# Attention state and ratio products of layer 0 over the value columns of their own half of the heads

## What is computed

```
Q = elu(xn @ wq.T + bq) + 1        K = elu(xn @ wk.T + bk) + 1        V = xn @ wv.T + bv
KV    = einsum('bhsd,bhse->bhde', K, V)       # per head: 16 x 16, summed over 512 tokens
K_sum = sum of K over the tokens              # per head: 16
out   = (Q @ KV) / (Q @ K_sum + 1e-8)         # per head
x    += out @ wo.T + bo + experts(xn)
```

## Time and profile before

| | |
|---|---|
| median of the runs | 1319.93 us |
| profiled execution, span | 1318.2 us |
| around the span (median less span) | 1.7 us |
| PE busy | 97% of the span |
| DVE, ACT, POOL busy | 60%, 40%, 10% |
| PE's share of the chain that ended last | 92% |

### The profile page before, as it was taken

One profiled execution on the slowest core, in us unless ns is written; L12 is line 12 of the kernel. 1 busy time (PEld: TensorE's weight loads), 2 busy tenths in 40 slices (PEclk: granted clock), 3 DMA queues, 4 the chain that ended last, 5 costly groups with the idle time before them and its releaser, 6 DMA issues.

```text
span 1318.2 us, 18254 instructions
## 1 busy us (share of the span) xinstructions
PE 1276.3 (97%) x5764; PEld 1027.9 (78%) x5764; DVE 793.0 (60%) x1522; ACT 520.8 (40%) x1030; POOL 134.3 (10%) x135
## 2 busy tenths in 40 slices
PE   3899999999999999999999999999999999999998
PEld 3687888888888888788888888888877778787775
DVE  6667667665555555667556555555674684544454
ACT  3344243343333333444433333333343433335332
POOL 2152232211000000020000000000102000001120
PEclk8999999999999999999999999999999999999999
DMA  4010110311111111111111111111210111001010
GB/s 166 14 40 27 40 41 26 103 39 53 52 39 51 52 52 44 34 40 53 53 52 39 52 52 52 39 51 52 66 38 25 37 37 38 25 25 38 25 57 32
DMA packets 29584, 60.95 MB, mean 46 GB/s; under 512 B 3490, under 2 KB 12124, under 8 KB 29276
## 3 DMA queue, kind: packets, MB, share of 16 engines
q1 hardware_dynamic: 29532, 60.28, 14.7%
HBM read 58.17 MB, written 2.10 MB: 46 GB/s over the span
## 4 chain that ended last, share of the span: by engine, by line
PE 92%; DVE 4%; ACT 2%; issue 1%; DMA 0%; POOL 0%; SPq 0%; DVEq 0%; ACTq 0%
PE banks L537 28%; PE banks L539 27%; PE banks L538 27%; PE banks L851 5%; PE banks L562 1%; PE banks L792 1%; DVE h_lo L1652 1%; PE banks L779 1%; PE banks L777 1%; DVE w_gu_lo L1339 1%; PE banks L773 1%; DMA x<-in_x_nat 0%; ACT L1004 0%; ACT h_hi L1166 0%; PE banks L657 0%
## 5 line engine op out<-in xcount | busy, mean ns | idle before, releaser
L537 PE MATMUL banks<-xn_hi,w_gu_hi 128*128 128x512 f32 x976 | 396.5, 406 | 10.4 <-DVE w_gu_lo L1339 10.4
L539 PE MATMUL banks<-xn_hi,w_gu_lo 128*128 128x512 f32 x976 | 385.1, 395 | 0.0
L538 PE MATMUL banks<-xn_lo,w_gu_hi 128*128 128x512 f32 x976 | 383.1, 393 | 0.0
L1636 DVE TENSOR_TENSOR gate<-gate,banks 128x512 f32<-128x512 f32 x244 | 167.7, 687 | 325.2 <-ACT gate L1155 319.5
L1155 ACT ACTIVATE gate<-banks 128x512 f32<-128x512 f32 x244 | 145.9, 598 | 402.3 <-PE banks L539 400.0
L1166 ACT CAST h_hi<-gate 128x512 fp32r<-128x512 f32 x244 | 151.4, 620 | 301.4 <-DVE gate L1641 301.3
L537 PEld LDWEIGHTS banks<-xn_hi,w_gu_hi 128*128 128x128 f32 x976 | 184.4, 189 | 59.8 <-issue 25.0
L1641 DVE TENSOR_TENSOR gate<-gate,banks 128x512 f32<-128x512 f32 x244 | 167.8, 688 | 96.7 <-PE banks L539 80.2
L539 PEld LDWEIGHTS banks<-xn_hi,w_gu_lo 128*128 128x128 f32 x976 | 184.1, 189 | 41.3
L538 PEld LDWEIGHTS banks<-xn_lo,w_gu_hi 128*128 128x128 f32 x976 | 184.8, 189 | 38.1 <-issue 1.1
L1652 DVE TENSOR_TENSOR h_lo<-gate,h_hi 128x512 fp32r<-128x512 f32 x244 | 170.1, 697 | 50.2 <-ACT h_hi L1166 42.9
(11 more groups left out here) (235 smaller groups left out, 978.6 us busy)
## 6 DMA issues: line engine op xcount, KB each, us to landing
w_raw<-in_moe SPq DMA_DIRECT2D x122, 384.0 KB
e_raw<-in_expand SPq DMA_DIRECT2D x94, 32.5 KB
x<-in_x_nat SPq DMA_DIRECT2D x4, 512.0 KB, 6.9
x<-in_x_t SPq DMA_DIRECT2D x1, 2048.0 KB, 9.2
out_t<-x SPq DMA_DIRECT2D x8, 256.0 KB, 2.5
w_raw<-in_w_attn SPq DMA_DIRECT2D x1, 1024.0 KB, 11.1
w_raw<-in_w_gla SPq DMA_DIRECT2D x1, 544.0 KB, 4.7
cst<-in_consts SPq DMA_DIRECT2D x1, 472.5 KB, 4.4
```

Of the source, the lines that this page charges most:

```text
L537: pe.matmul(out, wh[wsl], mh[msl], start=start, stop=False, skip_group_check=True)
L538: pe.matmul(out, wh[wsl], ml[msl], start=False, stop=False, skip_group_check=True)
L539: return pe.matmul(out, wl[wsl], mh[msl], start=False, stop=stop, skip_group_check=True)
L1636: v.tensor_tensor(gate[:, s, :], gate[:, s, :], bank[2][:], ALU.mult).then_inc(weighted, 1)
```

## The change

The state product of a half takes the value columns of that half alone, and the two columns of ones, 130 in all. For that the ones must stand beside either half: `kv_hi` and `kv_lo` get two more columns, and the layout becomes keys (256), ones (2), values (256), ones (2). Half 0 reads ones and values 0 to 127, half 1 reads values 128 to 255 and ones. `state` keeps per half 128 values and 8 sums (136 columns in place of 272). The ratio product writes the two halves beside each other in `side`, each as a sum of its own of three matmuls. `inv` becomes 2 x 8, and the DVE instructions of `ratio` read `side` in two pieces. The head selector in the constants shrinks from 32 to 8 columns.

```
+NH = P // HEAD
-C_ALL = C_HSEL + 2 * (D // HEAD)
-SW = D + D // HEAD
+C_ALL = C_HSEL + NH
+SW = P + NH
+KVW = 2 * D + 4
+V_AT = (D + 2, D + 2 + P)
+OWN_AT = (D, D + 2 + P)
...
-            kv_hi = sb0("kv_hi", [P, 4, 2 * D + 2], F32R)
-            kv_lo = sb0("kv_lo", [P, 4, 2 * D + 2], F32R)
+            kv_hi = sb0("kv_hi", [P, 4, KVW], F32R)
+            kv_lo = sb0("kv_lo", [P, 4, KVW], F32R)
...
-            inv = sb0("inv", [P, D // HEAD])
+            inv = sb0("inv", [P, 2, NH])
...
-            nc.gpsimd.memset(f(kv_hi[:, :, 2 * D:2 * D + 2]), 1.0).then_inc(const_made, 1)
-            nc.gpsimd.memset(f(kv_lo[:, :, 2 * D:2 * D + 2]), 0.0).then_inc(const_made, 1)
+            for at in (D, KVW - 2):
+                nc.gpsimd.memset(f(kv_hi[:, :, at:at + 2]), 1.0)
+                last = nc.gpsimd.memset(f(kv_lo[:, :, at:at + 2]), 0.0)
+                last.then_inc(const_made, 1)
...
                     v = (slice(None), t % 4, slice(D, 2 * D))
-                    split(kv_hi[v], kv_lo[v], kv[v], value_hi_done, t + 1)
+                    to = (slice(None), t % 4, slice(V_AT[0], V_AT[0] + D))
+                    split(kv_hi[to], kv_lo[to], kv[v], value_hi_done, t + 1)
...
-                    mm = three(side[:, 0:D + 2], (kv_hi, kv_lo), (everything, j, slice(hb * P, hb * P + P)),
-                               (kv_hi, kv_lo), (everything, j, slice(D, 2 * D + 2)), j == 0, j == 3)
+                    mm = three(side[:, 0:P + 2], (kv_hi, kv_lo), (everything, j, slice(hb * P, hb * P + P)),
+                               (kv_hi, kv_lo), (everything, j, slice(OWN_AT[hb], OWN_AT[hb] + P + 2)), j == 0, j == 3)
...
-                    mm = three(side[:, 0:SW], (q_hi, q_lo), (everything, hb, slice(j * P, j * P + P)),
-                               (state_hi, state_lo), (everything, hb, everything), hb == 0, hb == 1)
+                    mm = three(side[:, hb * SW:(hb + 1) * SW], (q_hi, q_lo), (everything, hb, slice(j * P, j * P + P)),
+                               (state_hi, state_lo), (everything, hb, everything), True, True)
...
-                v.tensor_tensor(state[:, hb, hb * P:hb * P + P], side[:, hb * P:hb * P + P],
-                                cst[:, C_HEADS:C_HEADS + P], ALU.mult)
-                own = C_HSEL + hb * (D // HEAD)
-                v.tensor_scalar(state[:, hb, D:SW], cst[:, own:own + D // HEAD], side[:, D:D + 1], None,
+                at, total = V_AT[hb] - OWN_AT[hb], (0, P)[hb]
+                v.tensor_tensor(state[:, hb, 0:P], side[:, at:at + P], cst[:, C_HEADS:C_HEADS + P], ALU.mult)
+                v.tensor_scalar(state[:, hb, P:SW], cst[:, C_HSEL:C_HSEL + NH], side[:, total:total + 1], None,
                                 ALU.mult).then_inc(state_masked, 1)
...
-                link(v.tensor_scalar(inv[:], side[:, D:SW], TINY, None, ALU.add))
+                both = side[:, 0:2 * SW].rearrange("p (a n) -> p a n", a=2)
+                link(v.tensor_scalar(inv[:], both[:, :, P:SW], TINY, None, ALU.add))
                 link(v.reciprocal(inv[:], inv[:]))
...
-                v.tensor_tensor(a_nat[:, t % 4].rearrange("p (h e) -> p h e", h=nh),
-                                side[:, 0:D].rearrange("p (h e) -> p h e", h=nh),
-                                inv[:].unsqueeze(2).to_broadcast([P, nh, HEAD]), ALU.mult).then_inc(attn_nat, 1)
+                v.tensor_tensor(a_nat[:, t % 4].rearrange("p (a h e) -> p a h e", a=2, h=NH),
+                                both[:, :, 0:P].rearrange("p a (h e) -> p a h e", h=NH),
+                                inv[:].unsqueeze(3).to_broadcast([P, 2, NH, HEAD]), ALU.mult).then_inc(attn_nat, 1)
```

More of the change, by code:

```diff
@@ L1394, in mask_state @@
                     dve.wait_ge(state_lo_done, b)
-                v.tensor_tensor(state[:, hb, hb * P:hb * P + P], side[:, hb * P:hb * P + P],
-                                cst[:, C_HEADS:C_HEADS + P], ALU.mult)
-                own = C_HSEL + hb * (D // HEAD)
-                v.tensor_scalar(state[:, hb, D:SW], cst[:, own:own + D // HEAD], side[:, D:D + 1], None,
+                at, total = V_AT[hb] - OWN_AT[hb], (0, P)[hb]
+                v.tensor_tensor(state[:, hb, 0:P], side[:, at:at + P], cst[:, C_HEADS:C_HEADS + P], ALU.mult)
+                v.tensor_scalar(state[:, hb, P:SW], cst[:, C_HSEL:C_HSEL + NH], side[:, total:total + 1], None,
                                 ALU.mult).then_inc(state_masked, 1)
             def ratio(t):
-                nh = D // HEAD
+                both = side[:, 0:2 * SW].rearrange("p (a n) -> p a n", a=2)
                 dve.wait_ge(ratio_mm, t + 1)
-                link(v.tensor_scalar(inv[:], side[:, D:SW], TINY, None, ALU.add))
+                link(v.tensor_scalar(inv[:], both[:, :, P:SW], TINY, None, ALU.add))
                 link(v.reciprocal(inv[:], inv[:]))
@@ L1688, in _constants @@
     c[:, C_START:C_START + SEQ] = np.arange(SEQ) % CH == 0
-    for hb in range(2):
-        heads = np.arange(D // HEAD)
-        c[:, C_HSEL + hb * len(heads):C_HSEL + (hb + 1) * len(heads)] = heads[None] == (hb * P + p[:, None]) // HEAD
+    c[:, C_HSEL:C_HSEL + NH] = np.arange(NH)[None] == p[:, None] // HEAD
     c[:, C_EPS] = LN_EPS
```

## The result

The changed kernel takes 1328.47 us (median of four runs, 1327.02 to 1328.85), against 1320.15 us for the kernel before beside it. The ratio is 1.006, interval [1.0046, 1.0074]: 8.3 us slower, and outside the predicted range. The profiled execution's span went from 1318.2 to 1326.9 us.

What follows compares the result with a forecast made beforehand. PE, busy for 97% of the span, was taken to bound the kernel. State products 0.8 us plus ratio products 0.3 us gave 1.1 us off 1319.93, so 1318.8 us; own-case range 1317.4 to 1321.4, overall range 1313 to 1322.5.

Steps and rivals of the forecast that it cites:

- The rest: Everything outside the narrowed matmuls (DVE reads, POOL splits, memsets, constants): taken as no gain or loss, constants under 0.1 us.
- Load-bound spacing: Narrowed state and ratio matmuls start every 0.1115 us, held by the next 128-column weight load; 1318.8 us, chance 0.70.
- rival of the plain rate: Narrow fp32r matmuls fall to plain float32's rate, 0.227 to 0.237 us each: +17.4 us, 1337.3 us; chance 0.17.
- unbound load: Weight load doesn't limit narrow matmuls: spacing 0.065 to 0.067 us, 1313.2 us (1315.2 with the page's 81 ns); chance 0.08.
- State products: 96 state matmuls, 258 to 130 columns, in units where PE never waits: all count, 0.8 us saved.
- Ratio products: 96 ratio matmuls, 272 to 136 columns: 72 in the first three groups worth nothing, last group's 24 save 0.3 us.
- The restart behind the gate product: Sign at PE's stop ahead of ratio product 2: PE restarts the same 6.7 us behind the gate product.
- The split reads at zero: DVE's inv and a_nat read in two pieces: no cost, at most 1.5 us; costlier rival 1322.4 us, chance 0.05.
- kv_hi, kv_lo keep their sizes: The splits into kv_hi and kv_lo keep their sizes, values moving by two columns; no time was added.
- the 1.1 us: Total forecast gain off the span: 0.8 us from state products plus 0.3 us from ratio products.
- The rivals: Alternatives: plain float32 rate (0.17), load not binding (0.08), costlier split reads (0.05); slower outcome 0.18 in all.

Runs made afterwards that it cites:

- e1: The changed kernel with 96 unused bytes a partition behind cst, so every tile behind cst has its place from before the change; 1318.83 us.
- e9: The changed kernel with 160 unused bytes behind cst, state products cut to 66 columns (batches 0, 2) or 64 weight columns (1, 3), sums incomplete; 1306.26 us.
- e11: The kernel before with 192 unused bytes a partition ahead of x and 64 behind cst, expert operands all at remainder 64 by 256; 1309.19 us.

## Why the prediction was wrong

- **The step that failed** is the last sentence of "The rest": "the constants are 12 KB smaller of 472.5, under 0.1 us". It priced the bytes of a transfer. The 96 bytes a partition also moved every tile behind cst, and this was costed at nothing because it wasn't looked at. It made each unit of the expert loops 53 to 60 ns longer. Between e1 and after, by the starts of the same matmuls, that is 3.3 and 4.2 us in the two loops and 1.7 outside them (the late first matmul of after and, against it, the dip of e1 at 68 us among them), 9.2 of span, and 9.6 by the medians of the runs. e1 takes it away alone and is at 1318.83 us.
- **Load-bound spacing, 0.1115 us:** right. It is 0.111 in the trace after, and e9 shows that the load is the limit and not the columns. The rival of the plain rate fell with it (0.22 us nowhere), and so did that of an unbound load, with 0.065 us as with 0.081 (for which its sum should have been 4.8 us, not 4.7).
- **State products, 0.8 us:** right. In e1 a product with its neighbours takes 1.58 us (81.13 to 82.71) in place of 1.67 (79.53 to 81.20), 0.09 on each of eight.
- **Ratio products, 72 of 96 absorbed, 0.3 us from the rest:** right. The restart behind the gate product stays at 6.7 us, and the last group keeps its 0.08 us a tile.
- **The split reads at zero:** right, 0.17, 0.26 and 0.42 us.
- **"kv_hi, kv_lo keep their sizes":** too short a look. The elements stayed, the stride didn't, and by POOL and DVE it gave back 0.4 of the 1.1 us. It wouldn't have taken the forecast out of its range. So even at the old places the sum lacked a term, and the median of e1 hides it.
- **The rivals** had a slower case of 0.18 in all, but by other mechanisms. None had the place of unchanged tiles, which no row of a single trace prices. The trace of before held a hint at most: gate and up matmuls at 228.8 ns and down matmuls at 231.5, the same instruction in the same clock at two speeds.

What stays open is why. A pair's remainders alone don't give its speed: the down matmuls have w 64 and h 64 both in the kernel before and in e11, where by 256 bytes only the tiles up to cst stand elsewhere, xn among them, and they start 231.5 and 226.7 ns apart. The padding moved operands of ScalarE, DVE and the DMA along with those of PE (gate, w_raw), so it isn't shown either that PE's own operands alone count. Every run with one remainder for all, at the one set of distances above, is fast: that much is shown and not the mechanism, nor why the loss is smaller in the stretch with attention (from e1 to after, 0.8 us between 77 and 278 us, some 45 units, in place of 2.7).

## What to carry to other kernels

Before and after an edit that resizes a tile, compare the places of all tiles behind it, and time the edit with padding that keeps them, or else the place is measured and not the edit. Where a kernel is bound by fp32r matmuls, try padding that brings the moving tiles and the weights to one remainder by 256 bytes, and measure it: here it was worth 0.7 to 0.8% for 64 bytes, some nine times the 1.1 us of the edit. And a narrower matmul stops paying where the next weight load takes longer than its columns.

## What the runs showed of the hardware

- A 512-column fp32r matmul starts every 226.7 to 234.3 ns on average over the gate, up and down matmuls, by nothing but unused bytes between the tiles, at a granted clock of 1.00 (2.4 GHz).
- With 128 columns of weights the spacing of fp32r matmuls has a floor of 0.111 us, the same at 130 and at 66 columns; with 64 columns of weights, 130 columns take 0.061.
- A POOL subtraction over 4 x 256 floats takes 2.20 us with rows 514 or 518 floats apart and 2.39 with 516. A DVE subtraction beside it waits it out: it ends 0.55 us behind it, and so takes 1.92 or 2.13 us in place of 0.69.
